# Two attention layers on one core: maxima copied in three parts, weighted sums copied between two exponentials, denominators turned by transposes

## What is computed

```python
w_attn = softmax(einsum('ncq,nck->nqk', q, k * scale), axis=2)   # over 2304 keys
a      = einsum('nqk,nck->ncq', w_attn, v)
out    = einsum('oc,bchw->bohw', proj_w, a) + proj_b + x
```

## Time and profile before

| | |
|---|---|
| median of 3 runs | 4348.03 us (4348.0 to 4350.7) |
| the profiled execution | 4349.48 us, of which its span is 4347.7 us |
| busy share of the span: PE, DVE, ACT, POOL | 95%, 74%, 64%, 33% |
| work of the two attention stages | 96 blocks, 576 steps of three slots |

### The profile page before, as it was taken

The page is one execution under the profiler, slowest core; times in us unless marked ns, Lnnn a source line. Parts: engine busy times, 40 slices in busy tenths (PEclk is TensorE's granted clock), DMA queues, the critical chain, the costliest instruction groups (busy, mean ns, idle before and its releaser), DMA issues. The chain is left out here.

```text
span 4347.7 us, 87107 instructions
## 1 busy us (share of the span) xinstructions
PE 4111.5 (95%) x30264; PEld 1954.1 (45%) x30264; DVE 3208.9 (74%) x3852; ACT 2767.8 (64%) x2789; POOL 1443.2 (33%) x584
## 2 busy tenths in 40 slices
PE   7998999999999999998999989999999999999989
PEld 4554444444444444444555544444444444444445
DVE  3112899999999999998322239999999999999972
ACT  1112788888888888886000018888888888888850
POOL 0000444444444444444100004444444444444430
PEclk9999999999999999999999999999999999999999
DMA  4212000100000000011323320101000000000116
GB/s 171 78 74 85 8 30 16 34 14 29 22 25 22 22 24 24 25 47 39 125 100 127 105 78 10 35 13 31 20 27 22 22 22 23 25 20 29 40 44 210
DMA packets 157931, 208.40 MB, mean 48 GB/s; under 512 B 9008, under 2 KB 144304, under 8 KB 156848
## 3 DMA queue, kind: packets, MB, share of 16 engines
q1 hardware_dynamic: 137712, 179.28, 12.5%
q10 hardware_dynamic: 20160, 28.32, 1.8%
HBM read 113.19 MB, written 94.37 MB: 48 GB/s over the span
## 5 line engine op out<-in xcount | busy, mean ns | idle before, releaser
L586 POOL TENSOR_TENSOR prob<-prob,mx 128x1056 f32<-128x1056 f32 x576 | 1422.3, 2469 | 2743.4 <-DVE prob L586 2743.4
L749 ACT ACTIVATE prob<-psum_att 128x768 f32<-128x768 f32 x1728 | 1386.3, 811 | 1062.2 <-PE psum_att L679 539.7
L690 PE MATMUL psum_att<-prob,vst 128*32 128x384 f32 x13824 | 1237.6, 491 | 92.1 <-ACT pvr L769 70.1
L679 PE MATMUL psum_att<-qst,kst 64*128 64x384 f32 x6912 | 1288.2, 505 | 30.1 <-DMA kst<-qk_scratch 18.0
L848 DVE TENSOR_TENSOR run<-psum_att,run 128x768 f32<-128x768 f32 x1344 | 1224.3, 948 | 58.5 <-PE psum_att L679 53.7
L763 ACT ACTIVATE prob<-prob 128x2304 f32<-128x2304 f32 x576 | 1220.2, 2119 | 19.9 <-POOL prob L586 19.9
L586 DVE TENSOR_TENSOR prob<-prob,mx 128x1248 f32<-128x1248 f32 x576 | 859.1, 1492 | 76.8 <-ACT mx L756 76.8
L679 PEld LDWEIGHTS psum_att<-qst,kst 64*128 64x128 f32 x6912 | 625.0, 188 | 518.9 <-ACT prob L749 142.3
L690 PEld LDWEIGHTS psum_att<-prob,vst 128*32 128x32 f32 x13824 | 396.7, 110 | 848.5 <-issue 698.9
L860 DVE TENSOR_TENSOR two_tiles<-prob 128x768 f32<-128x768 f32 x576 | 577.7, 1003 | 1.4 <-ACT prob L763 1.3
L309 PE MATMUL psum<-xc_l,wq 128*128 128x384 f32 x1536 | 504.7, 490 | 9.6 <-DVE qk_l L406 4.4
(11 more groups left out here) (54 smaller groups left out, 1593.2 us busy)
## 6 DMA issues: line engine op xcount, KB each, us to landing
qk_scratch<-qk_l SPq DMA_DIRECT2D x48, 768.0 KB, 3.5
v_scratch<-vo_l SPq DMA_DIRECT2D x24, 768.0 KB, 3.6
qst<-qk_scratch SPq DMA_DIRECT2D x96, 192.0 KB, 2.4
kst<-qk_scratch SPq DMA_DIRECT2D x96, 192.0 KB, 2.4
vst<-v_scratch SPq DMA_DIRECT2D x96, 192.0 KB, 2.5
att_scratch<-ob ACTq DMA_DIRECT2D x96, 192.0 KB, 1.9
attc_l<-att_scratch SPq DMA_DIRECT2D x24, 768.0 KB, 5.4
x_sb<-in_x SPq DMA_DIRECT2D x8, 1152.0 KB, 14.0
```

What stands on the lines that cost most here:

```text
L586: return engine.tensor_tensor(x, x, m, ALU.subtract)
L679: mm = nc.tensor.matmul(psum[:, 2 * k + e, 0:CH], kst[rows, (3 * c + k) * P:(3 * c + k + 1) * P], qst[par][rows, :], start=True, stop=True ...
L690: mm = nc.tensor.matmul(psum[d:d + 32, 6, 0:CH], vst[:, kt, d:d + 32], prob[par][:, d // D, kt, :], start=(kt == 0), stop=(kt == KT - 1), ...
L749: nc.scalar.activation(prob[par][:, :, s, :], s_banks(k)[:, :, 0:CH], ACT.Copy).then_inc(copied, 1)
```

## The change

The maxima are copied in three parts of 128 x 256, each behind the copy of the slot that uses the same two banks; `mx_ready` now counts three for each block, and PE waits for the parts in `bank_free` instead of `spare_free`. The exponential of a step is two instructions, one for each head, and `copy_weighted` stands between them, in step 3 instead of ahead of the copies of step 4. `weigh` and `pair_tiles` wait for both halves. `turn_den` is three transposes into the spare strips of banks 3, 4 and 5, without the constant `heads`; DVE therefore adds the two partial sums itself, in two small reductions (`sum_den`, bank 3 ahead of the maximum of the step's second slot, banks 4 and 5 ahead of the third), and `invert` waits for these on its own engine.

```diff
-PV_COPY_AT, DEN_COPY_AT, DEN_TURN_AT, DEN_SPREAD_AT, STORE_AT = 4, 5, 2, 3, 3
+PV_COPY_AT, DEN_COPY_AT, DEN_TURN_AT, DEN_SPREAD_AT, STORE_AT = 3, 5, 2, 3, 3
...
             def bank_free(t, c, k):
                 if c > 0 or not before(t, 1):
                     pe.wait_ge(copied, slot(t, 3 * (c - 1) + k) if live(t) else slot(NB - 1, KT - 1))
+                if c == BROADCAST_AT + 1 and not before(t, 1) and live(t - 1):
+                    pe.wait_ge(mx_ready, 3 * (t - 1) + k + 1)
 
             def spare_free(t, c):
-                if c == BROADCAST_AT + 1 and not before(t, 1) and live(t - 1):
-                    pe.wait_ge(mx_ready, t)
                 if c == DEN_TURN_AT + 1 and not before(t, 3) and live(t - 3):
-                    pe.wait_ge(inverted, t - 2)
+                    pe.wait_ge(den_summed, 2 * (t - 2))
...
                 for r in range(3):
-                    mm = nc.tensor.matmul(psum[:, 5, CH + 2 * r:CH + 2 * r + 2], den[:, r * P:(r + 1) * P], heads,
-                                          start=True, stop=True)
+                    mm = nc.tensor.transpose(psum[:, 3 + r, CH:512], den[:, r * P:(r + 1) * P], ident)
                 mm.then_inc(den_turned, 1)
...
-                pe.wait_ge(exp_done, group(t, c))
+                pe.wait_ge(exp_done, 2 * group(t, c))
...
+            def copy_max(t, par, r):
+                if r == 0:
+                    act.wait_ge(broadcast, t + 1)
+                    if not before(t, 2):
+                        act.wait_ge(dve_shifted, group(t - 2, KC - 1))
+                        act.wait_ge(pool_shifted, group(t - 2, KC - 1))
+                nc.scalar.activation(mx[par][:, :, r * P:(r + 1) * P], s_banks(r)[:, :, CH:512], ACT.Copy)\
+                    .then_inc(mx_ready, 1)
+
+            def exponential(t, par, c, e):
                 act.wait_ge(dve_shifted, group(t, c))
                 act.wait_ge(pool_shifted, group(t, c))
-                x = prob[par][:, :, 3 * c:3 * c + 3, :]
+                x = prob[par][:, e, 3 * c:3 * c + 3, :]
                 nc.scalar.activation(x, x, ACT.Exp, scale=SCALE).then_inc(exp_done, 1)
...
-                    if c == PV_COPY_AT and not before(t, 2) and live(t - 2):
-                        copy_weighted(t - 2)
...
                         if live(t):
                             copy(t, par, 3 * c + k)
-                    if c == BROADCAST_AT and not before(t, 1) and live(t - 1):
-                        copy_max(t - 1, 1 - par)
-                    if live(te):
-                        exponential(te, pe_, ce)
+                        if c == BROADCAST_AT and not before(t, 1) and live(t - 1):
+                            copy_max(t - 1, 1 - par, k)
+                    for e in range(2):
+                        if live(te):
+                            exponential(te, pe_, ce, e)
+                        if e == 0 and c == PV_COPY_AT and not before(t, 2) and live(t - 2):
+                            copy_weighted(t - 2)
...
-            def invert(t):
+            def sum_den(t, k):
+                parts = slice(0, 1) if k == 1 else slice(1, 3)
                 dve.wait_ge(den_turned, t + 1)
                 if live(t + 3):
-                    dve.wait_ge(scored, scored_count(slot(t + 3, 3 * DEN_TURN_AT + 2)))
+                    dve.wait_ge(scored, scored_count(slot(t + 3, 3 * DEN_TURN_AT + k)))
+                if not before(t, 1):
+                    dve.wait_ge(inverted, t)
+                groups = psum[:, 3:6, CH:512].rearrange("p r (e o i) -> p r e o i", e=2, o=2)[:, parts, :, :, 0]
+                nc.vector.tensor_reduce(dsum[:, parts, :], groups, AX.X, ALU.add).then_inc(den_summed, 1)
+
+            def invert(t):
+                dve.wait_ge(den_summed, 2 * (t + 1))
                 if not before(t, 1):
                     dve.wait_ge(widened, t)
-                nc.vector.reciprocal(dcol[:, :, :], psum[:, 5, CH:CH + 6].rearrange("p (r e) -> p r e", r=3))\
-                    .then_inc(inverted, 1)
+                nc.vector.reciprocal(dcol[:, :, :], dsum[:, :, :]).then_inc(inverted, 1)
```

More of the change, by code:

```diff
@@ L526, in attention_stage @@
         run, fold, mx, mcol = bufs["run"], bufs["fold"], bufs["mx"], bufs["mcol"]
-        den, dcol, dwide = bufs["den"], bufs["dcol"], bufs["dwide"]
+        den, dsum, dcol, dwide = bufs["den"], bufs["dsum"], bufs["dcol"], bufs["dwide"]
         pvr, ob, two_tiles = bufs["pvr"], bufs["ob"], bufs["two_tiles"]
-        ones, heads, ident = bufs["ones"], bufs["heads"], bufs["ident"]
+        ones, ident = bufs["ones"], bufs["ident"]
         q_in = [sem(f"q_in{p}") for p in range(2)]
@@ L545, in attention_stage @@
         den_copied, pv_copied = sem("den_copied"), sem("pv_copied")
-        den_turned, inverted = sem("den_turned"), sem("inverted")
+        den_turned, den_summed, inverted = sem("den_turned"), sem("den_summed"), sem("inverted")
         widened, spread = sem("widened"), sem("spread")
@@ L821, in _ @@
                         if c == 0:
-                            pool.wait_ge(mx_ready, t + 1)
+                            pool.wait_ge(mx_ready, 3 * (t + 1))
                         pool.wait_ge(copied, slot(t, 3 * c + 2))
@@ L856, in pair_tiles @@
             def pair_tiles(t, par, c):
-                dve.wait_ge(exp_done, group(t, c))
+                dve.wait_ge(exp_done, 2 * group(t, c))
                 if c >= 2 or not before(t, 1):
@@ L864, in shift @@
                 if c == 0:
-                    dve.wait_ge(mx_ready, t + 1)
+                    dve.wait_ge(mx_ready, 3 * (t + 1))
                 dve.wait_ge(copied, slot(t, 3 * c + 2))
                 shift_part(nc.vector, par, c, 0, SHIFT_DVE).then_inc(dve_shifted, 1)
-            def invert(t):
+            def sum_den(t, k):
+                parts = slice(0, 1) if k == 1 else slice(1, 3)
                 dve.wait_ge(den_turned, t + 1)
                 if live(t + 3):
-                    dve.wait_ge(scored, scored_count(slot(t + 3, 3 * DEN_TURN_AT + 2)))
+                    dve.wait_ge(scored, scored_count(slot(t + 3, 3 * DEN_TURN_AT + k)))
[5 more added lines that the diff above has]
+                dve.wait_ge(den_summed, 2 * (t + 1))
                 if not before(t, 1):
                     dve.wait_ge(widened, t)
-                nc.vector.reciprocal(dcol[:, :, :], psum[:, 5, CH:CH + 6].rearrange("p (r e) -> p r e", r=3))\
-                    .then_inc(inverted, 1)
+                nc.vector.reciprocal(dcol[:, :, :], dsum[:, :, :]).then_inc(inverted, 1)
             def norm(t, par, r):
@@ L892, in body @@
                             reduce(t - 1, k)
-                        if c == DEN_TURN_AT and k == 2 and not before(t, 3) and live(t - 3):
-                            invert(t - 3)
+                        if c == DEN_TURN_AT and k > 0 and not before(t, 3) and live(t - 3):
+                            sum_den(t - 3, k)
+                            if k == 2:
+                                invert(t - 3)
                         if c == DEN_SPREAD_AT and not before(t, 3) and live(t - 3):
@@ L921, in program @@
     with ExitStack() as ctx:
-        const_sb = sb_(ctx, nc, "const_sb", [P, 32 + 2 + 2 * P])
+        const_sb = sb_(ctx, nc, "const_sb", [P, 32 + 2 * P])
         par_sb = sb_(ctx, nc, "par_sb", [P, 2 * CT + 2 * CT + CT + CT])
-        ones, heads = const_sb[:, 0:32], const_sb[:, 32:34]
-        gmat, ident = const_sb[:, 34:34 + P], const_sb[:, 34 + P:34 + 2 * P]
+        ones, gmat, ident = const_sb[:, 0:32], const_sb[:, 32:32 + P], const_sb[:, 32 + P:32 + 2 * P]
         par = {"gn_w": par_sb[:, 0:CT], "gn_b": par_sb[:, CT:2 * CT], "qkv_b": par_sb[:, 2 * CT:4 * CT],
@@ L968, in attention @@
                         "mx": two("mx", [P, 2, CH]), "mcol": sb_(c2, nc, f"mcol_{layer}", [P, 2, 3]),
-                        "den": sb_(c2, nc, f"den_{layer}", [P, CH]), "dcol": sb_(c2, nc, f"dcol_{layer}", [P, 3, 2]),
+                        "den": sb_(c2, nc, f"den_{layer}", [P, CH]), "dsum": sb_(c2, nc, f"dsum_{layer}", [P, 3, 2]),
+                        "dcol": sb_(c2, nc, f"dcol_{layer}", [P, 3, 2]),
                         "dwide": sb_(c2, nc, f"dwide_{layer}", [P, 3, P]), "pvr": sb_(c2, nc, f"pvr_{layer}", [P, CH]),
                         "ob": two("ob", [P, CH]), "two_tiles": two("two_tiles", [P, 2, CH]),
-                        "ones": ones, "heads": heads, "ident": ident}
+                        "ones": ones, "ident": ident}
                 attention_stage(nc, f"att{layer}", psum, bufs, qk_d, v_d, att_d, next_loads)
@@ L1038, in constants @@
     f = np.float32
-    heads = np.zeros((P, 2), f)
-    for e in range(2):
-        heads[64 * e, e] = heads[64 * e + 32, e] = 1
     g = np.kron(np.eye(P // GROUP, dtype=f), np.full((GROUP, GROUP), 1.0 / GROUP, f))
-    return np.ascontiguousarray(np.concatenate([np.ones((P, 32), f), heads, g, np.eye(P, dtype=f)], 1))
+    return np.ascontiguousarray(np.concatenate([np.ones((P, 32), f), g, np.eye(P, dtype=f)], 1))
```

## The result

The changed kernel takes 4303.8 us (median of 4 runs, 4296.8 to 4304.7) against 4348.6 us; the ratio is 0.9893 with a 95% interval from 0.9876 to 0.991. That is 44.7 us faster, 1.0% by the medians and 1.1% by the ratio, where 4313 us had been predicted, 35 us faster. Its profiled execution took 4302.96 us with a span of 4301.2 us.

A forecast was written before the change was run, and what follows sets the result against it. PE, busy 95% of the span, was taken as the bound, through its meetings with ACT and DVE. Terms of -0.30, -0.26, +0.25 and -0.07 gave -0.38 us a block, -35 us over 93 blocks: 4313 us, range 4285 to 4350.

The forecast's parts named there:

- The maxima in three parts: Step 1: the last part ends 0.13 us earlier and PE's release comes 0.17 sooner, together -0.30 us a block.
- the place of the wait: Step 1: waiting for the maxima behind the slot copy's wait, not first of three, starts PE 0.17 us sooner.
- The turn: Step 2 on PE: three transposes take 0.48 us to the next scores instead of 0.74, -0.26 us a block.
- The sums on DVE: Step 2: two reductions delay the third slot's copy, so PE is later at `spread_den`: +0.25 us a block.
- The mechanism: Step 2: 0.21 us on ACT before the third slot's copy is the only cover for DVE's delay at `spread_den`.
- `weigh` in step 4: PE's stall stays but waits for the exponential's second half instead of the weighted sums' copy: mean -0.07 us a block.
- Both stalls go: Rival: PE's stalls at the denominators' turn and at `weigh` vanish, -1.53 us a block, 4206 us; chance 0.04.
- The sum: Whole block: -0.30 - 0.26 + 0.25 - 0.07 = -0.38 us, over 93 blocks -35 us.
- No change: Rival: PE's releases at the turn and `weigh` stay slow and the sums cost +0.31 us, 4348 us; chance 0.13.
- Slower: Rival: step 2's reductions at 0.42 us make PE 0.77 us later at `spread_den`, 4361 us; chance 0.10.
- The drain: Rival: step 2's first reduction and reciprocal each hold DVE 0.18 us, not 0.10: -0.22 a block, 4328 us; chance 0.08.

The follow-up runs named there:

- the run with the slot ahead of the turn: Changed kernel with PE taking the first slot's scores of step 2 ahead of the turn of the denominators: 4293.1 us.
- the edit on ACT: Changed kernel with step 2's first slot's scores ahead of the denominators' turn, plus, on ACT, each part of the maxima ahead of its slot's copy: 4265.0 us.

## Why the prediction was right, point by point

- **The maxima in three parts: -0.30 us a block.** Right in both halves. The timeline has 5.29 us from the scores to the turn against 5.59, and the run of this part alone gave -28.7 us, or -0.31 a block. The 0.17 us for the place of the wait, which the prediction took from another wait in the same place, were tested by moving the wait and hold (15 us of 93 x 0.17 = 16).
- **The turn: -0.26.** Right, 0.48 against 0.74 us. In the run of this part alone it was 0.45 (1010.55 to 1011.00). The waits for the parts ahead of the scores, which the prediction put at nothing, are the likely reason for the 0.03 us; that was not tried apart.
- **The sums on DVE: +0.25 was the term that was mis-sized.** It measured +0.13, at the low end of its bounds (+0.12), and the stall ahead of `spread_den` is 0.16 us and not 0.28. The prediction leaned to two additions that did not come: 0.08 us for a second wait at `invert`, where the row shows 0.03 us in all, and up to 0.11 more for the maximum behind the reciprocal, which follows 0.11 us after the reciprocal's start where 0.10 to 0.21 had been allowed. The mechanism (cover of 0.21 us on ACT, then PE pays in full) was right, by the run with one sum taken twice: +19.5 us for some 0.2 us of DVE.
- **`weigh` in step 4: -0.07 on the mean.** Right; -6.4 us alone. That the stall would stay and change its releaser, from the copy to the second half, was right, and so was the start of `weigh` 0.06 us behind it (1015.35 against a half's end at 1015.29). "Both stalls go" is out by the same rows.
- **The sum.** With +0.13 for the sums it is -0.30 - 0.26 + 0.13 - 0.07 = -0.50 us a block, 93 x -0.50 = -46.5 us; measured are -44.7. So the 10 us by which the forecast fell short are, within the noise, the sums on DVE. The prediction's own bounds were added up wrongly: with the turn and `weigh` they give -0.92 to -0.15 us a block, and not -0.65 to -0.10. The range of times reached to 4350 us, so it would have held for no change as well; what bears the account is the terms.
- **The rivals.** "No change" needed slow releases behind the last part and the second half; they were 0.05 and 0.06 us. "Slower" needed reductions of 0.42 us; they take 0.15 and 0.16. The drain is out as well: the reduction takes 0.15 us and the maximum starts 0.07 us after the reduction's start. The section of the Trainium skill that was weighed for it ("VectorE: DVE Perf Modes", "The DRAIN you can't avoid") says in the same place that a next operation which is not held starts earlier. The prediction left that out; these rows agree with it.
- **What the prediction missed** without harm to its number: it said that DVE waits for PE in every step of the stretch, so that delays don't pile up. The earlier turn used that up in step 2, where DVE's idle 0.44 us became nothing. By the terms as they stand it cost nothing yet, but a further 0.44 us won on PE alone brings next to nothing, as the run with the slot ahead of the turn shows (-11.5 us instead of -41).

## What to carry to other kernels

Price an edit at the points where the bounding engine meets the others, and ask at each what is late next: here the copy of the weighted sums gave way to the exponential just behind it, and the gain was 6 us and not 70. When a filled stall gives nothing, look for a second chain from the same source; step 2 hung on the last part of the maxima through PE and through DVE, and the edit on PE paid only with the edit on ACT. Count also what a new order costs the bounding engine itself: the turn between two slots' scores took 0.20 us more. Of several waits ahead of one instruction, try the one that comes true last nearest to it; here that was worth 15 us.

## What the runs showed of the hardware that I had not expected

A DVE operation whose two inputs both lie in SBUF becomes longer while POOL works on SBUF, and one with an input in PSUM does not. With POOL busy for 3.09 us, `pair_tiles` took 1.47 us instead of 0.95 and the fold 1.35 instead of 0.96, while the three maxima under the same POOL instruction took 2.68 us, as without it. The kernel before already shows it once a block: beside POOL's subtraction its `pair_tiles` of step 0 takes 1.17 us.

```profile
1003.75 1.17 DVE L860 TENSOR_TENSOR two_tiles<-prob 128x768 f32<-128x768 f32 x1
```

The Trainium skill says as much in "SBUF — State Buffer", section "Who interferes with whom": a VectorE instruction with two SBUF inputs contends with a GpSimd instruction that reads SBUF, one with at most one SBUF input, outside the two-port modes, does not. These rows agree.

The order of three waits on PE that all have to be met moved its start by 0.20 us (0.05 against 0.25 us behind the last one). And the parts of one copy were not equal: 0.38, 0.40 or 0.41 and 0.43 us for the same 128 x 256 where each stands behind its slot's copy, 0.38, 0.39 and 0.42 where each stands ahead of it; what makes the later ones longer was not tried.
